# One product per token tile turns the row maxima of four heads together, and the keys carry four groups of three selecting rows

## The reference

```python
q = q * cos + rotate_half(q) * sin
k = k * cos + rotate_half(k) * sin
scores = jnp.einsum('bhqd,bhkd->bhqk', q, k) * scale
scores = jnp.where(causal[None, None], -jnp.inf, scores)
attn = jax.nn.softmax(scores, axis=-1)
out = jnp.einsum('bhqk,bhkd->bhqd', attn, v)
...
x = x + attention(xn) + experts(xn)      # experts: gate, top 4 of 8 groups, top 6 experts, plus a shared part
```

## Time and profile before

| | |
|---|---|
| median of 3 runs (lowest, highest) | 900.64 us (897.58, 901.23) |
| the profiled execution's own time | 899.4 us |
| its span | 897.6 us, mean granted TensorE clock 0.975 |
| TensorE busy | 828.9 us (92%) |
| VectorE busy | 605.0 us (67%) |
| ScalarE busy | 493.1 us (55%) |
| GpSimd busy | 503.7 us (56%) |

### The profile page before, as it was taken

One profiled execution on the slowest core, in us unless ns is written; L12 is line 12 of the kernel. 1 busy time (PEld: TensorE's weight loads), 2 busy tenths in 40 slices (PEclk: granted clock), 3 DMA queues, 4 the chain that ended last, 5 costly groups with the idle time before them and its releaser, 6 DMA issues.

```text
span 897.6 us, 17583 instructions
## 1 busy us (share of the span) xinstructions
PE 828.9 (92%) x5281; PEld 454.0 (51%) x5282; DVE 605.0 (67%) x1187; ACT 493.1 (55%) x1214; POOL 503.7 (56%) x651
## 2 busy tenths in 40 slices
PE   5799987788989999999999999999999999999997
PEld 2366654233343443378888888873344343433444
DVE  2577776878877788755555555557788777888322
ACT  3466543144646566644444444547676766667662
POOL 3556650399889821066667666526888888820000
PEclk9799988789999999999999999999999999999999
DMA  7015545620000041047778777784585555510011
GB/s 226 1 38 178 190 149 160 171 65 19 1 19 1 14 119 47 1 131 250 220 219 245 231 231 231 135 144 72 71 173 90 73 89 71 89 25 1 13 36 48
DMA packets 81986, 96.15 MB, mean 107 GB/s; under 512 B 13030, under 2 KB 73446, under 8 KB 81894
## 3 DMA queue, kind: packets, MB, share of 16 engines
q0 software_dynamic: 19968, 31.47, 19.6%
q1 hardware_dynamic: 45033, 46.80, 17.4%
q10 hardware_dynamic: 16896, 16.78, 5.5%
HBM read 61.11 MB, written 33.82 MB: 106 GB/s over the span
## 4 chain that ended last, share of the span: by engine, by line
PE 77%; DVE 12%; issue 4%; DMA 2%; DVEq 2%; SPq 1%; ACT 1%; POOLq 1%; POOL 1%; ACTq 0%
PE bank L1201 14%; PE bank L1184 13%; PE vector_banks L1276 12%; PE vector_banks L1160 11%; DVE mpart L958 8%; PE vector_banks L1052 6%; PE bank L1293 6%; PE vector_banks L1073 4%; PE bank L1073 3%; PE bank L1052 2%; DMA xn_all<-wexp 2%; PE vector_banks L1221 2%; PE vector_banks L1163 1%; PE bank L1187 1%; PE bank L1089 1%
## 5 line engine op out<-in xcount | busy, mean ns | idle before, releaser
L958 DVE TENSOR_REDUCE mpart<-vector_banks 128x2 f32<-128x1024 f32 (+3 forms) x320 | 330.0, 1062 | 82.1 <-PE vector_banks L1160 50.6
L716 ACT ACTIVATE probs<-bank 128x512 f32<-128x512 f32 (+3 forms) x428 | 212.3, 539 | 129.8 <-PE bank L1184 65.9
L1184 PE MATMUL bank<-turned 99*128 99x512 bf16 (+3 forms) x640 | 201.2, 353 | 7.7 <-DVE turned L980 2.2
L1160 PE MATMUL vector_banks<-turned 96*128 96x512 bf16 (+3 forms) x640 | 184.7, 358 | 13.2 <-DVE mpart L958 12.3
L589 POOL DMA_INDIRECT turned<-normed_rows,tok_i x128 | 125.3, 979 | 122.3 <-PE vector_banks L1052 89.1
L604 POOL DMA_INDIRECT res<-expert_rows,slot_i x96 | 148.8, 1550 | 41.4 <-issue 28.4
L716 ACT ACTIVATE at_first<-bank 128x512 f32<-128x512 f32 (+3 forms) x212 | 105.6, 533 | 71.8 <-PE bank L1187 39.1
L1184 PEld LDWEIGHTS bank<-turned 99*128 99x128 bf16 x640 | 58.3, 97 | 164.5 <-ACT probs L716 71.3
L1276 PE MATMUL vector_banks<-xn_all,probs 128*128 x512 | 135.2, 386 | 4.6 <-issue 1.6
L1201 PE MATMUL bank<-probs,V 128*32 128x512 f32 (+3 forms) x856 | 102.5, 550 | 0.0
L1276 PEld LDWEIGHTS vector_banks<-xn_all,probs 128*128 128x128 f32 x512 | 87.1, 190 | 17.4 <-issue 9.7
(11 more groups left out here) (154 smaller groups left out, 983.6 us busy)
## 6 DMA issues: line engine op xcount, KB each, us to landing
expert_rows<-probs ACTq DMA_DIRECT2D x32, 512.0 KB, 4.4
term_rows<-at_first SPq DMA_DIRECT2D x96, 128.0 KB
turned<-term_rows SPq DMA_DIRECT2D x32, 384.0 KB, 4.4
xn_all<-wexp SPq DMA_DIRECT2D x32, 384.0 KB, 4.0
normed_rows<-xn_all SPq DMA_DIRECT2D x4, 512.0 KB, 5.7
turned<-normed_rows,tok_i POOLq DMA_INDIRECT x128, 4.1
out<-res SPq DMA_DIRECT2D x16, 128.0 KB, 1.7
res<-x SPq DMA_DIRECT2D x1, 1536.0 KB, 8.9
```

Of the source, the lines that this page charges most:

```text
L716: A(PT[v // 2 % 6][:, v % 2, 0:width], bank[A_BANK[step][0]][:, 0:width], ACT.Exp).then_inc(s["scalar_bank_read"], 1)
L958: V.tensor_reduce(mpart[:, t % TPC, 2 * j:2 * j + 2, p], ring[:, :, 0:w], AX.X, ALU.max).then_inc(s["vector_bank_read"], 1)
L1160: last = mm(ring[:, h, 0:w], q_turned(slice(0, KQ), 2 * j + h, t * P, P), k_turned(par, slice(0, KQ), 2 * j + h, p * CH, w), start=True, s ...
L1184: last = mm(ring[:, 0:CH - off], k_turned(parity(g), slice(0, KM), h, kb * P, P), q_turned(slice(0, KM), h, c * CH + off, CH - off), start ...
```

## The change

The key rows behind row 95 become twelve, three per head, and for head h only its own three are ones; the other nine are zeros. The queries of every head carry the maxima parts of all four heads in these twelve rows. So `mcat`'s 4 heads x 3 parts of one token tile are turned by one product with 12 weight columns, and an `mt` step issues 4 products in place of 16. VectorE's copy reads the 512 turned columns once per head (a repeated read) and writes 12 rows in place of 3. The pattern of ones and zeros is a new tile `own_rows` that GpSimd makes at the start, ahead of `ident_made`, by one memset and two selects; SyncE puts it into the keys by four DMAs, one per head. The later copy to the other parity takes 12 rows.

```diff
-KM = KQ + 3
+KM = KQ + 3 * HG
...
+        own_rows = before([P, HG, P], BF16)
...
             sp.wait_ge(s["ident_made"], 1)
-            sp.dma_start(QK[KQ:KM, HG * T:2 * HG * T].rearrange("p (a n) -> p a n", n=P),
-                         onesb[0:KM - KQ, :].unsqueeze(1).to_broadcast([KM - KQ, HG * T // P, P])).then_inc(s["ones_made"], 16)
+            for h in range(HG):
+                sp.dma_start(k_turned(0, slice(KQ, KM), h, 0, T).rearrange("p (a n) -> p a n", n=P),
+                             own_rows[0:KM - KQ, h:h + 1, :].to_broadcast([KM - KQ, T // P, P])).then_inc(s["ones_made"], 16)
...
-            sp.wait_ge(s["ones_made"], 16)
+            sp.wait_ge(s["ones_made"], 16 * HG)
...
+            gp.memset(own_rows[:, :, :], 1.0)
...
+            gp.affine_select(out=own_rows[:, :, :], in_=own_rows[:, :, :], compare_op=ALU.is_ge, fill=0.0, base=0,
+                             pattern=[[-3, HG], [0, P]], channel_multiplier=1)
+            gp.drain()
+            gp.affine_select(out=own_rows[:, :, :], in_=own_rows[:, :, :], compare_op=ALU.is_ge, fill=0.0, base=2,
+                             pattern=[[3, HG], [0, P]], channel_multiplier=-1)
+            gp.drain()
             gp.tensor_copy(tile_at[:, :], tile_i[:, :]).then_inc(s["ident_made"], 1)
...
                         V.tensor_copy(QK[KQ:KM, 0:HG * T].rearrange("p (h q) -> p h q", q=T)[:, :, c * CH:(c + 1) * CH],
-                                      ring[KQ:KM, :, :].rearrange("p a b -> p (a b)").bitcast(BF16).rearrange("p (h q) -> p h q", q=CH)
+                                      ring[KQ:KM, 0, :].bitcast(BF16)[:, 0:CH].unsqueeze(1).to_broadcast([KM - KQ, HG, CH])
...
-                        for j in range(HG):
-                            for t in range(TPC):
-                                k = j % 2 * TPC + t
-                                last = turn(ring[KQ:KM, j // 2, :].bitcast(BF16)[:, k * P:(k + 1) * P],
-                                            mcat[:, t * HG + j, :], identb[:, :])
+                        for t in range(TPC):
+                            last = turn(ring[KQ:KM, 0, :].bitcast(BF16)[:, t * P:(t + 1) * P],
+                                        mcat[:, t * HG:(t + 1) * HG, :].rearrange("p h i -> p (h i)"), identb[:, :])
```

More of the change, by code:

```diff
@@ L1179, in attend @@
                             if c == 0 and g == 0:
-                                pe.wait_ge(s["ones_made"], 16)
+                                pe.wait_ge(s["ones_made"], 16 * HG)
                             if c == 0 and g == 1:
```

## The result

The changed kernel took 889.58 us in the median of 4 runs (888.71 to 890.38), the kernel before 899.11 us beside it (4 runs): ratio 0.9901, 95% interval 0.9874 to 0.9927, 9.5 us less. Run again later beside other runs of the kernel before it took 888.43 us against 898.01, ratio 0.989 (0.986 to 0.992), 9.6 us less. The prediction was 891.5 us.

The account below looks back on a forecast made before the run. TensorE was taken to bound the kernel, with 77% of the chain and VectorE a close second in attention. Savings of 6.7 + 2.0 + 0.5 = 9.2 us from 899.4 gave 890.2, or 891.4 from the median; predicted 891.5 us, range 887 to 899.5.

Parts of the forecast that it names:

- The size: Whole kernel: 9.2 us saved, summed over the 16 `mt` steps as 6.7 + 2.0 + 0.5.
- the prediction's own signs: Wrong if above 896 us with copy at 1.23, or gains far from 5 us up to 385 us, 4 in late attention.
- Twelve products fewer, 0.67 us a step: TensorE's `mt` steps: starts 0.055 us apart, so twelve fewer save 0.67 us each, 1.3 at lower clock; ceiling 11.3 us.
- What stays, by class of step: `mt` steps by VectorE's work beside the products: nine keep 6.7 us, three 2.0, three 0.5, the one at 214 us 0.
- the 298 us step: One of three `mt` steps (298, 639, 757 us) whose reduction ends with the products; each keeps 0.67 us on TensorE.
- the covered 335 us step: One of three `mt` steps (335, 674, 791 us) whose reduction starts with the products; each keeps 0.16 us.
- The copy: VectorE's copy in `mt` steps stays at 1.23 us despite the repeated read; cost 0, bounds 0 and +1.2 us each.
- The rival's price: Slow copy in `mt`: +1.2 us a step, 19.4 us on VectorE, three quarters on the path, 906 us; chance 0.06.
- The start: GpSimd's added constants take 2.05 us, `ident_made` comes at 9.1 us, hidden behind other work; cost 0, at upper bound 0.25 us.
- SyncE's queue: One issue of 0.96 us at 11.12 becomes four, up to 3.8 us; cost 0, upper bound 0.5 us.
- VectorE absorbs it: Attention: VectorE sets the pace, TensorE only reaches its reduction waits earlier; only 2.7 us gained, 898 us; chance 0.20.
- The clock: TensorE's low-clock part, 152 to 188 us, lengthens or shortens by 4 us: 895 or 887 us; chance 0.09, both directions.

Follow-up runs that it names:

- e11: The kernel before, unchanged, run again for a second profile: 900.10 us, ratio 1.0019 against the same kernel.
- e8: The changed kernel, unaltered, run again for a second profile: 888.43 us.
- e1: The changed kernel with each of the four products of an `mt` step issued four times, 16 in all: 897.46 us, ratio 0.9978 to the kernel before.
- e2: The changed kernel with each of the four products of an `mt` step issued seven times, 28 in all: 905.42 us, ratio 1.0071 to the kernel before.
- e12: The kernel before with head 0's four products issued four times, 28 products a step in place of 16: 907.25 us, ratio 1.0100.
- e3: The changed kernel with VectorE's copy of each `mt` step done twice, a drain between: 908.67 us, ratio 1.0110 to the kernel before.
- e9: On top of e4, head groups 1 to 3: VectorE copies two heads, ScalarE the other two four places later in the order: 890.59 us, ratio 0.9915.
- e4: The changed kernel with GpSimd making the pattern rows behind `ident_made` and VectorE's last statistics step, with their own semaphore: 888.21 us, ratio 0.9865.

## Why the prediction was right, point by point

- **The size.** 9.5 us measured (9.6 in the repeat), 9.2 predicted. The sum is closer than its parts, and that is partly luck. By the table's columns the 9.2 us are 2.0 ahead of the third copy, 2.8 in the third column, 0.7 in the experts' and 3.7 in the last. The two pairs of profiles (before and changed, e11 and e8) gave 4.9 and 4.8, 1.6 (with its dip of the clock) and 3.0, 1.7 and 4.4, 2.7 and 3.2. By the prediction's own signs, up to 385 us it gave back 6.5 and 7.9 us, more than the 5 named, and late attention less than 4.
- **Twelve products fewer, 0.67 us a step.** Right. Products with 12 weight columns last 0.220 us for 0.219, four of them 0.39 us, and e1, e2 and e12 show that TensorE's time for them is the gain: 7.9 us for the twelve, where the sum had 9.2, a difference inside the noise of the medians. The Trainium skill's 81 ns a product (page "TensorE: Matmul & The Clock Gate", section "Back-to-back issue gap") does not hold in these bursts: 0.63 to 0.67 us for twelve more are 53 to 56 ns each.
- **What stays, by class of step.** Right in early attention at full clock: 3.0 us in the third column, 2.8 by the classes. Against the profile before, the copies move as the classes say in most places. The copy at 272.6 moved 0.66 us forward beyond the one ahead of it; that at 336.1, behind the 298 us step, 0.67; that at 381.6, behind the covered 335 us step, 0.83, just 0.16 + 0.67. In late attention the steps at 639 and 757 us kept 0.36 and 0.29 us, not 0.67 (0.26 and 0.49 between the repeats); the step at 732 us kept 0.38, but 0.80 between the repeats. There the sum of 3.7 us came out as 2.7 and 3.2. So the term that was too large is what the covered steps of late attention keep, by 0.5 to 1.0 us. TensorE, ahead by 0.67, met the next reduction sooner: the waits at other ring steps rose by 1.4 and 1.7 us.
- **The copy.** Right on its time (1230 ns). The rival's price, three quarters of an added time on the path, is near e3's four fifths at full clock and under its medians (19 of 20.8 us). By these two shares a copy slower by 19.4 us in all would have ended between 905 and 907.5 us, an estimate; the rival had 906. The rule of the Trainium skill (page "VectorE: DVE Perf Modes", section "What auto-detection actually checks"), that 16-bit tensors with step 1 keep the doubled rate, agrees with this row, which has a repeated source.
- **The start.** A step that failed, though small. I costed the selects by their length alone (0.65 us each; they took 0.63) and by what waits for `ident_made` (it came at 9.08 us, predicted 9.1). I left out what they do beside them: two of VectorE's steps took 0.55 and 0.45 us in place of 0.16, the scales came late, the first turn started at 10.04. 0.6 us at the start, predicted 0.
- **SyncE's queue.** The four issues took 3.51 us and nothing waited for them: cost 0, as predicted.
- **VectorE absorbs it.** It did so by about a quarter of what the products took in steps at full clock (12 x 0.67 = 8.0 us, of which e1 against e8 shows 6.0), not by all but 2.7 us in the whole. The 80% of busy time spoke for the rival, the 50 us that VectorE idles for score products against it, and these were the better guide.
- **The clock.** The part ahead of the third copy gave 4.9 us in the first comparison and 4.8 in the repeat, for 2.0 by the products. The layout alone can't be the cause: e12 has the old one, twelve products more a step, and its third copy at 212.8, ahead of both profiles of before. e1 with its 16 products has it at 209.9, e2 with 28 at 215.0. The clock granted between 152 and 188 us was 0.67 in both profiles of before and from 0.66 to 0.81 in the others, but e8 with 0.67 has the copy as early as the first profile with 0.81, so this stretch alone doesn't settle it. Where the low-clock stretches fall, from 30 us on, is the likely cause; no run isolates it, and it stays open. The medians' gain isn't from this: the ten runs of the changed kernel and the 62 of the kernel before have the same mean granted clock, 0.974. e1 ends 2 us below the kernel before, within its interval; the experts' column, shorter by 1.9 and 3.8 us at equal products, can hold that.

## What to carry to other kernels

- Where TensorE leads the chain, small products count by the distance between their starts, not by their duration: 16 products of 0.22 us were 1.05 us, and twelve fewer took 0.67 us off a step, of which three quarters reached the end. Here a product with 12 weight columns cost what one with 3 does (0.220 and 0.219 us).
- Time added to an engine that is second in the chain can still cost most of itself: four fifths of the doubled copy at full clock. A share handed to a third engine must not make that engine wait in its order.
- Compare distances between landmarks, and look at the granted clock in each before reading a difference of 2 us. Here one dip made 3.0 us look like 1.6, and another made up 1.8 of e9's 2.7.

## What the runs showed of the hardware

- VectorE's steps of four elements a row took 0.55 and 0.45 us in place of 0.16 while GpSimd ran a select of 512 elements a row; the one that fell between two selects took 0.16 us, and with the selects moved away both took 0.17. Both long steps ended 0.02 us behind the select. Selects of 128 elements can do it too: in e4 a step of 0.17 took 0.32 us beside one.
- A 16-bit copy from PSUM that reads the same 512 values four times takes 1230 ns for 2048 values, exactly what it takes without repeating, in 12 rows as in 3. ScalarE takes 1052 ns for 1024 such values from SBUF, VectorE 697 ns from PSUM.
- In 62 runs of one kernel the time went with the mean granted clock, from 893.6 us at 0.983 to 905.3 at 0.964, 0.62 us for each 0.001.
